# A transformer block's causal attention: two heads per step in blocks of 256 queries, and two heads' weights per product

## The reference

```
latent = xn @ Wkv_down                       # 64 numbers per token; xn = layernorm(x)
q, k, v per head (64 wide); k = latent @ Wk_up, v = latent @ Wv_up
attn = softmax(where(causal, q @ k.T / 8, -inf))
x = x + (attn @ v) @ Wout                    # summed over the 16 heads
x = x + ffn(layernorm(x))                    # 6 experts, top 2, and a shared one; two rounds
```

## Time and profile before

| | |
|---|---|
| median of three runs | 2874.68 us |
| the profiled execution | 2871.32 us, its span 2868.5 us |
| busy: PE, DVE, POOL, ACT | 2681.7, 1975.1, 1933.7, 1724.2 us |
| mean granted clock | 0.958 |
| first score matmul, last score matmul | 96.3 us, 1839.6 us |

### The profile page before, as it was taken

One profiled execution on the slowest core, in us unless ns is written; L12 is line 12 of the kernel. 1 busy time (PEld: TensorE's weight loads), 2 busy tenths in 40 slices (PEclk: granted clock), 3 DMA queues, 4 the chain that ended last, 5 costly groups with the idle time before them and its releaser, 6 DMA issues. The chain is left out here.

```text
span 2868.5 us, 47472 instructions
## 1 busy us (share of the span) xinstructions
PE 2681.7 (93%) x13656; PEld 2222.5 (77%) x13656; DVE 1975.1 (69%) x4387; ACT 1724.2 (60%) x4016; POOL 1933.7 (67%) x1735
## 2 busy tenths in 40 slices
PE   7999999999989999999999999799989998879994
PEld 5688888888777888888878888688878887768873
DVE  6688788887887788788887887255744464753455
ACT  2577777777776777777777777633323442224442
POOL 2598998998878888988988989722442232543224
PEclk8799999999999999999999999899999998879997
DMA  3011111111111010111110100154333451224552
GB/s 71 14 40 47 39 40 47 36 33 43 36 42 36 25 27 22 27 33 25 27 33 24 23 23 21 46 178 135 118 125 122 139 151 55 94 98 142 178 164 91
DMA packets 162064, 191.53 MB, mean 67 GB/s; under 512 B 57996, under 2 KB 126866, under 8 KB 161304
## 3 DMA queue, kind: packets, MB, share of 16 engines
q1 hardware_dynamic: 148504, 154.67, 18.6%
q0 software_dynamic: 12288, 33.57, 3.6%
q10 hardware_dynamic: 1024, 0.26, 0.0%
HBM read 114.45 MB, written 83.14 MB: 69 GB/s over the span
## 5 line engine op out<-in xcount | busy, mean ns | idle before, releaser
L305 POOL TENSOR_TENSOR pl<-pr,ph 128x512 fp32r<-128x512 f32 (+3 forms) x1184 | 1373.9, 1184 | 211.2 <-ACT ph L723 189.4
L720 ACT ACTIVATE pr<-ps 128x512 f32<-128x512 f32 (+3 forms) x1280 | 688.0, 538 | 401.6 <-PE ps L473 161.6
L995 DVE TENSOR_REDUCE part<-ps 128x1 f32<-128x512 f32 (+3 forms) x1152 | 704.0, 617 | 137.7 <-PE ps L458 122.5
L723 ACT ACTIVATE ph<-ps 128x512 fp32r<-128x512 f32 (+3 forms) x1280 | 686.7, 537 | 0.0
L458 PE MATMUL ps<-k_hi,q_parts 128*128 128x512 f32 (+3 forms) x1280 | 493.2, 386 | 41.5 <-DVE part L995 36.1
L472 PE MATMUL ps<-q_parts,k_hi 128*128 128x512 f32 (+3 forms) x1280 | 482.5, 377 | 0.3
L473 PE MATMUL ps<-q_row,k_lo 65*128 65x512 f32 (+3 forms) x1280 | 471.3, 368 | 0.0
L458 PEld LDWEIGHTS ps<-k_hi,q_parts 128*128 128x128 f32 x1280 | 243.8, 191 | 137.1 <-DVE part L995 57.9
L472 PEld LDWEIGHTS ps<-q_parts,k_hi 128*128 128x128 f32 x1280 | 242.1, 189 | 55.5 <-ACT ph L723 7.6
L473 PEld LDWEIGHTS ps<-q_row,k_lo 65*128 65x128 f32 x1280 | 242.7, 190 | 34.1
L1895 POOL DMA_INDIRECT x_slots<-xcur,slot_i x128 | 126.1, 985 | 167.7 <-PE ps L1615 80.4
(11 more groups left out here) (251 smaller groups left out, 4680.1 us busy)
## 6 DMA issues: line engine op xcount, KB each, us to landing
work<-x_slots SPq DMA_DIRECT2D x148, 128.0 KB
...
rec<-recip_rows SPq DMA_DIRECT2D x128, 128.0 KB
y_latent<-y_sums SPq DMA_DIRECT2D x128, 128.0 KB
...
```

The costliest lines, as they stand in the source:

```text
L305: eng.tensor_tensor(pl[:, s % RING, 0:w], pr[:, s % PR_RING, 0:w], f32(ph[:, s % RING, 0:w]), ALU.subtract).then_inc(sem, 1)
L720: act.activation(pr[:, s % PR_RING, 0:w], src, ACT.Exp).then_inc(S["probs"], 1)
L723: act.activation(ph[:, s % RING, 0:w], src, ACT.Exp).then_inc(S["probs_hi"], 1)
L995: ins = dve.tensor_reduce(dst, src[:, 0:w], AX.X, ALU.max)
```

## The change

A step takes both heads of a pair side by side, 256 queries of each, with one tile of keys. There are 8 blocks (`b`), block b has 2b+2 steps, 72 in a pair, of which the last two lie on the diagonal; all are 512 columns wide, except the very last of a block, which is 2 x 128. One mask instruction covers both heads. The query buffers of the two heads become one with the heads interleaved in blocks of 256. Maxima are still 80 matmuls a pair, but a row of keys is cut into even parts (9 tiles as 3, 3, 3 and not 4, 4, 1), and they run 27 ahead, 80 of them over 72 steps, so that every ninth step has two. VectorE does `make_lo` in every ninth step, eight in a pair. All tables of steps are new. SP's queue takes the four transfers of a block's normalization at steps of their own rather than one block's after another, with a semaphore for each of four buffers; results are stored for both heads at once.

At the start, the weights are loaded with the two heads of a pair on 128 partitions; the ones that are multiplied lie in blocks on the diagonal of a 128 x 128 matrix that VectorE has cleared, so that one product gives both heads. In `make_m` 16 products of 128 columns replace 32 of 64; in `make_n` 8 of 256 replace 16.

```diff
-SCORE_STEPS = [(qb, kt) for qb in range(QB) for kt in range(TPB * (qb + 1))]
-MAX_STEPS = [(TPB * qb + j, c) for qb in range(QB) for j in range(TPB) for c in range(qb + 1)]
-STEPS = len(SCORE_STEPS)
-INVERT_AFTER = 8
-DIVIDE_AFTER = 13
+QW = BLK // 2
+NB = L // QW
+
+
+def even_parts(n):
+
+    k = -(-n // TPB)
+    sizes = [n // k + (c < n % k) for c in range(k)]
+    return [(sum(sizes[:c]), sizes[c]) for c in range(k)]
+
+
+SCORE_STEPS = [(b, kt) for b in range(NB) for kt in range(2 * b + 2)]
+MAX_STEPS = [(b, head, j, c, at * P, n * P) for b in range(NB) for head in range(2) for j in range(2)
+             for c, (at, n) in enumerate(even_parts(2 * b + j + 1))]
+STEPS, MAXES = len(SCORE_STEPS), len(MAX_STEPS)
+LEAD = 27
+COPY_AFTER, INVERT_AFTER, DIVIDE_AFTER = 6, 9, 14
+SUMS_AFTER, RECIP_AFTER, SPREAD_AFTER, STORE_AFTER = 7, 10, 12, 15
...
-BANK_JOBS = [(1, "row", 0, 3), (5, "row", 1, 0), (8, "proj", 2, 0), (13, "row", 1, 1), (16, "proj", 2, 1),
...
-SPLITS = [(6, 1, 3), (9, 2, 0), (17, 2, 1), (29, 2, 2), (44, 2, 3), (47, 3, 0), (54, 3, 1), (66, 3, 2)]
...
+BANK_JOBS = [(10, "row", 0, 4), (15, "proj", 1, 0), (20, "row", 0, 5), (27, "proj", 1, 1), (35, "row", 0, 6), (41, "proj", 1, 2),
...
+SPLITS = [(2, 0, 3, 0), (5, 0, 3, 1), (18, 1, 0, 0), (21, 1, 0, 1), (30, 1, 1, 0), (33, 1, 1, 1), (44, 1, 2, 0), (47, 1, 2, 1)]
...
-ON_DVE = [s % STEPS in (10, 20, 30) for s in range(2 * STEPS)]
-DVE_LOS, POOL_LOS = sum(ON_DVE), 2 * STEPS - sum(ON_DVE)
+ON_DVE = [s % 9 == 4 for s in range(STEPS)]
+DVE_LOS, POOL_LOS = sum(ON_DVE), STEPS - sum(ON_DVE)
...
+def width(s):
+
+    b, kt = SCORE_STEPS[s]
+    return BLK if kt <= 2 * b else BLK // 2
...
+def maxes_at(s, p):
+
+    steps = range(LEAD + MAXES * s // STEPS, LEAD + MAXES * (s + 1) // STEPS)
+    return [(p + n // MAXES, n % MAXES) for n in steps if p + n // MAXES < TURNS]
...
+                def store(p, b):
+                    sp.wait_ge(S["normed"], 8 * p + b + 1)
+                    rows = y_dram[p // PAIRS][b // 2, :, p % PAIRS, QW * (b % 2):QW * (b % 2 + 1)].rearrange("(h d) n -> d h n", h=2)
+                    sp.dma_start(rows, halves(y[0:LD, b % QB, :])).then_inc(S[f"stored{b % QB}"], DMA)
...
+                def load_two(to, of, pairs, sem):
+
+                    for half in range(2):
+                        rows = slice(half * HD, (half + 1) * HD)
+                        src = w[of].rearrange("(a two) k c -> two k a c", two=2)[half]
+                        cols = slice(0, D) if src.shape[-1] == D else slice(half * LD, (half + 1) * LD)
+                        sp.dma_start(to[rows, pairs, cols], src[:, pairs, :]).then_inc(sem, DMA)
...
-                def max_scores(half, m, split_no, n, seq, first=False):
-                    i, c = MAX_STEPS[m]
-                    if c == 0 and i % TPB == 0:
-                        pe.wait_ge(S["q_hi"], split_no + 1)
-                        pe.wait_ge(S["q_lo"], split_no + 1)
-                        pe.wait_ge(S["k_hi"], QB * seq + i // TPB + 1)
+                    pe.transpose(ps[0:TPB, BANK, 0:P], mx[:, b % 2, :], T["ident"][:, :]).then_inc(S["bank_made"], 1)
+
+                def max_scores(pair, m, first=False):
+                    b, head, j, c, at, w = MAX_STEPS[m]
+                    n, seq = MAXES * pair + m, pair // PAIRS
+                    if c == 0 and j == 0:
+                        no = split_no(pair, b // 2, head)
+                        pe.wait_ge(S["q_hi"], no + 1)
+                        pe.wait_ge(S["q_lo"], no + 1)
+                        if head == 0:
+                            pe.wait_ge(S["k_hi"], QB * seq + b // 2 + 1)
                     if not first:
                         pe.wait_ge(S["max_read"], n - 1)
-                    w = BLK if c < i // TPB else P * (i % TPB + 1)
-                    pe.matmul(ps[:, MAX_BANK + m % 2, 0:w], qa[half][:, i * P:(i + 1) * P],
-                              khs[seq][:, c * BLK:c * BLK + w], start=True, stop=True).then_inc(S["max_scored"], 1)
-
-                def scores(half, m, s, p, first, last):
-                    qb, kt = SCORE_STEPS[m]
-                    off = P * max(0, kt - TPB * qb)
+                    pe.matmul(ps[:, MAX_BANK + n % 2, 0:w], qa[:, b, head, j * P:(j + 1) * P],
+                              khs[seq][:, at:at + w], start=True, stop=True).then_inc(S["max_scored"], 1)
...
+                def scores(s, p, first):
+                    b, kt = SCORE_STEPS[s]
+                    off = 0 if kt <= 2 * b else P
                     if kt == 0:
-                        pe.wait_ge(S["q_copy"], 8 * p + 4 * half + qb + 1)
-                        pe.wait_ge(S[f"row_in{qb}"], DMA * (2 * p + half + 1))
+                        pe.wait_ge(S["q_copy"], split_no(p, b // 2, 1) + 1)
+                        pe.wait_ge(S[f"row_in{b % QB}"], DMA * (2 * p + b // QB + 1))
                     if not (first and s < 3):
-                        pe.wait_ge(S["probs_hi"], 2 * STEPS * p + same_bank_before(s) + 1)
-                    out = ps[:, SCORE_BANK + s % 3, 0:BLK - off]
-                    q = slice(BLK * qb + off, BLK * (qb + 1))
+                        pe.wait_ge(S["probs_hi"], STEPS * p + s - 2)
+                    out = halves(ps[:, SCORE_BANK + s % 3, 0:width(s)])
                     k = slice(kt * P, (kt + 1) * P)
-                    pe.matmul(out, khs[p // PAIRS][:, k], qa[half][:, q], start=True, stop=False)
-                    pe.matmul(out, kls[p // PAIRS][0:LD + 1, k], qc[half][:, q], start=False, stop=True).then_inc(S["scored"], 1)
+                    pe.matmul(out, khs[p // PAIRS][:, k], qa[:, b, :, off:QW], start=True, stop=False)
+                    pe.matmul(out, kls[p // PAIRS][0:LD + 1, k], qc[:, b, :, off:QW], start=False, stop=True).then_inc(S["scored"], 1)
...
+                    out = halves(ps[:, Y_BANK + b % 2, :])[:, :, off:QW]
+                    hi, lo = halves(ph[:, s % RING, 0:w]), halves(pl[:, s % RING, 0:w])
                     v_hi, v_lo = vas[p // PAIRS], vcs[p // PAIRS]
-                    pe.matmul(out, v_hi[:, kt, :], ph[:, b, 0:w], start=kt == 0, stop=False)
-                    pe.matmul(out, v_lo[:, kt, :], ph[:, b, 0:w], start=False, stop=False)
-                    pe.matmul(out, v_hi[:, kt, :], pl[:, b, 0:w], start=False,
-                              stop=kt == TPB * (qb + 1) - 1).then_inc(S["latent_used"], 1)
+                    pe.matmul(out, v_hi[:, kt, :], hi, start=kt == 0, stop=False)
+                    pe.matmul(out, v_lo[:, kt, :], hi, start=False, stop=False)
+                    pe.matmul(out, v_hi[:, kt, :], lo, start=False, stop=kt == 2 * b + 1).then_inc(S["latent_used"], 1)
...
-                    for s in range(2 * STEPS):
-                        half, m = s // STEPS, s % STEPS
-                        if not (last and half == 1):
-                            split_no = 8 * p + 4 * (half + 1) + MAX_STEPS[m][0] // TPB
-                            max_scores(1 - half, m, split_no, STEPS + 2 * STEPS * p + s, (p + half) // PAIRS)
-                        for job, (_, kind, head, qb) in jobs_at(s, p):
+                    for s in range(STEPS):
+                        for pair, m in maxes_at(s, p):
+                            max_scores(pair, m)
...
+                        mm = pe.matmul(ps[:, M_BANKS[a], col:col + P], wq[:, pair, dt * P:(dt + 1) * P], wk[:, pair, :],
                                        start=True, stop=True)
...
-                    half, two = h % 2, h // 2 % 2
-                    mm = pe.matmul(ps[half * LD:(half + 1) * LD, N_BANKS[a], two * D:(two + 1) * D],
-                                   wv[:, h, :], wo[:, h, :], start=True, stop=True)
-                    if h % 4 == 3:
+                    mm = pe.matmul(ps[:, N_BANKS[a], two * D:(two + 1) * D], wv[:, pair, :], wo[:, pair, :], start=True, stop=True)
...
-                    early, late = first_max_steps(g)
-                    for n, m in enumerate(early + late):
-                        max_scores(0, m, g, m, 0, first=m < 2)
...
-                        if g == 3:
-                            make_n(n)
...
+                turn_latents(3)
+                make_n(0)
+                make_n(1)
+                for m in range(24, LEAD):
+                    max_scores(0, m)
+                    make_n(2 * (m - 24) + 2)
+                    make_n(2 * (m - 24) + 3)
+                    if m == 25:
+                        first_row(3)
...
+                    src = halves(ps[:, SCORE_BANK + s % 3, 0:w])[:, :, 0:P]
+                    dve.wait_ge(S["scored"], STEPS * p + s + 1)
+                    dve.tensor_tensor(src, src, T["mask_kq"][:, None, :].broadcast_to([P, 2, P]), ALU.add).then_inc(S["masked"], 1)
```

590 lines of the change are left out of this document (298 added, 292 removed).

## The result

The changed kernel takes **2901.98 us** (median of four, 2893.23 to 2911.03) against 2872.66 of the kernel before (2867.48 to 2879.78): **1.0105 times as long, 95% interval 1.0082 to 1.0128**. Forecast was 2812. That is 1% slower, where the prediction gave faster 0.92. Chips differ by over 1% (the kernel before took 2842 us on one and 2881 on another), so what follows compares ratios, or pairs of heads in the trace.

What follows compares the result with a forecast made beforehand. TensorE's columns were taken to bound the kernel, 95% of a pair, the rest stalls. Ordinary pairs −34, pairs 6 and 7 −8, last pair 0, start −20 sum to −62 us: 2812 us, range 2776 to 2858.

Steps and rivals of the forecast that it cites:

- TensorE's need: Ordinary pair of heads: TensorE's work without stalls falls by 1.5 to 100.8 us, as fewer narrow matmuls remain.
- The stalls: Ordinary pair: TensorE's waiting put at 4.5 us, from 5.6 measured before, with ends of 2 and 8.
- The bunch: Step 5 of a pair: mask, masked maximum, split and subtraction give VectorE 3.9 us against TensorE's 0.8; lateness lasts four steps.
- The end of 8: Upper end for stalls a pair: three bunches pass through with 1.5 us each on top of most of today's.
- Rival D: Ordinary pairs: VectorE's subtractions hold GpSimd, its work becomes 104.6 us, a pair some 107; 2835 us in all; chance 0.03.
- DMA: SP's queue: interleaved normalization transfers and 1 KB result pieces cost nothing; a late transfer would delay division and copy of sums.
- Pairs 6 and 7: Pairs where the second sequence is prepared: 125 and 113 us expected, −8 together, from 0 to −16.
- The start: Before the first score: fewer products in make_n and make_m at the lower clock save −20 us, from −14 to −26.
- Rival F: The start does not shorten, VectorE's layer norm setting it and the clock staying low: −8 not −20, 2824 us; chance 0.06.
- B: Ordinary pairs: the stalls dissolve to 2 us a pair; 2780 us, about 2775 with a better pair 6; chance 0.14.
- C: Ordinary pairs: the bunches of VectorE work bite, 8 us of stalls a pair; 2857 us, still faster; chance 0.09.
- E: Slower: masks behind bunches hold ScalarE and score banks; 9.3 us of stalls cancel the gain, 12 give 2910 us; chance 0.06.

Runs made afterwards that it cites:

- Experiment 1: Changed kernel with the second maximum of a two-maximum step issued behind the weights' products: 0.988 of the kernel before, in repeated rounds 0.9912 [0.9889, 0.9935].
- experiment 3: Changed kernel with two query splits moved, from step 5 to 7 and from 33 to 37: 2862.79 us, 0.994 of the kernel before.
- experiment 6: On top of experiment 4, splits and VectorE's subtractions put at steps chosen by a sum of its work against TensorE's: 2781.57 us, 0.979 of the kernel before.
- experiment 2: Changed kernel with SP's queue issuing the clearing of slots three steps later: 2879.77 us, 0.9996 of the kernel before.
- experiment 4: Changed kernel with the edits of Experiment 1, experiment 2 and experiment 3 together: 2826.43 us, 0.981 of the kernel before.
- experiment 5: On top of experiment 4, the second sequence's normalisations one tile a step, its jobs clear of rows and projections: 2782.28 us, 0.979 of the kernel before.
- experiment 7: The edits of experiment 5 and experiment 6 together, on top of experiment 4: 2755.26 us, 0.969 of the kernel before.
- experiment 9: On top of experiment 7, the second sequence's moments and GpSimd's step on them earlier: 2782.13 us, 0.9651 [0.9625, 0.9676] of the kernel before.
- experiment 8: Changed kernel with VectorE setting masks behind the maximum reads at diagonal steps: 2871.61 us, 1.0103 of the kernel before.
- experiment 11: The changed kernel again, unchanged, in rounds on one chip: 1.0081 [1.0054, 1.0108] of the kernel before.

## Why the prediction was wrong

*TensorE's need*: right. 100.8 us forecast, 100.8 to 101.0 found in every version (pairs of 110.2 to 103.8 us less the stalls of each). Of the 84 us between the forecast −62 and the +21.9 of the profiled execution, about 60 lie in the 13 ordinary pairs, 33 in pairs 6 and 7 and 6 in the last; the start gave 11 back and the rest 5.

*The stalls*: **the step that failed.** 4.5 us a pair were taken, 8.1 to 10.3 came, and "two maximum banks and three score banks absorb two to three steps of lateness" was the sentence behind it. I had counted banks, not maxima. 80 maxima in 72 steps were in the same text as a sum of columns, and not as eight steps with two, where two banks cover one step of lateness and not two. The bunch was counted, 3.9 us of VectorE's work against 0.8 of TensorE's; that is 3.1 us, over two of TensorE's steps of 1.4, and so at the edge of what a single maximum allows. In pair 9 it holds one for 1.1 us, though it is shorter than counted. Experiment 1 takes 2.6 of the 8.1 us away by moving the second maximum alone; experiment 3 takes 1.7 by dissolving two bunches; VectorE's plan of experiment 6 on top leaves 2.9. The end of 8 given for bunches passing through was the value that came in pairs 8 to 14, without the double steps that made part of it.

*VectorE and GpSimd*: the prices erred to the safe side. The wide mask took 0.428 (0.43 forecast), the split 0.62 (0.99), the subtraction 1.15 (1.58), and the bunch of step 5 is 3.3 us in pair 9 (its split takes 0.90) and not 3.9, and VectorE does 84 to 86 us and not 89. It was less work than forecast and still more waiting: where it stood counted. Rival D is out: GpSimd's mean of 1.34 stayed, its work is 92.5. But the reading that VectorE pays for the overlap and GpSimd does not is wrong. The earlier trace rows show the two GpSimd instructions up to the end of the wait; the next, 128x384 at 668.46, took 1.45 us, where that shape's mean is 1.09. The last section has the measure of it.

*DMA*: "nothing booked" was wrong where slots are cleared. The prediction named the consequence of a late transfer, and did not look for what stands between the moved steps on SP's queue. Moving the clearing took 1.9 us off each of pairs 1 to 5 (experiment 2, one trace), 9 in all.

*Pairs 6 and 7*: 125 and 113 forecast, 142.4 and 128.7 came, the largest single miss. I had argued from the amount of VectorE's work (109.3, forecast 110) as a lower bound and expected the pair near it. Stalls there were 37.9 and 21.2 us (24.3 and 7.2 before), some of them clock: pair 6 was granted 0.93 where it had 0.96. Experiments 4, 5 and 7 bring the stalls to 20.9 and 5.8 and the pairs to 125 and 113.5, by the same edits as in ordinary pairs and by jobs set apart. What holds the last 20 us of pair 6 stays open: experiment 9 took one suspected wait away and gained 1.4.

*Last pair*: 0 forecast, +6.3 in the profile (98.2 us at a granted clock of 0.97). In experiment 2, whose edit does not reach this pair, it took 94.6 at 1.00, so more than half of the excess goes with the lower clock; 93.7 and 96.2 in experiments 8 and 11, 92.2 in experiment 9.

*The start*: −20 forecast, −30.8 found, outside its range. The products were as few as described, and the clock rose as I had not booked: TensorE was granted 0.50 through the last 40 us before, and 0.83 in the last 40 us now, 1.00 in the last 8.5:

```profile
57.00:65.50 8.50, 5.25 (x27) 4.13 (x26) 6.60 (x14) 3.80 (x8) 1.27 (x1) 1.00 0.00 0
25.40:65.50 40.10, 27.14 (x124) 20.78 (x123) 31.43 (x64) 14.67 (x30) 10.20 (x8) 0.83 0.00 1
```

The eight products with their maxima, from 57.84 us on, took 4.4 us where 10.8 were forecast at the lower clock. TensorE then stood idle for 3.0 us, for which the profile names no releaser:

```profile
65.20 0.47 PE L497 MATMUL ps<-k_hi,q_parts 128*128 128x512 f32 x1 [3.00 <-issue]
```

Rival F is out. What makes the clock rise earlier I did not test, nor how the 11 us divide between it and the work.

*The rivals*: B did not come; experiment 6 brought the stalls to 2.9, near its 2. C's price (8 a pair) is what late pairs did; with 125 and 113 us for pairs 6 and 7 it would have been 2857. E has the right sign and place on the scale (9.3 us of stalls a pair to cancel the gain; the mean of pairs 1 to 5 and 8 to 14 was 9.0), and the wrong mechanism: ScalarE's waits for masks fell, if only to 8.1 us a pair, and experiment 8 made every mask later at no cost that the total shows. Its chance of 0.06 was far too low, since all of what could make stalls was argued from the kernel before, where no bunch of this height and no double step stood: there no step of a late pair stalls for more than 0.9 us.
